# Three edits to a four-layer attention kernel: gates between layers 0 and 1, a mask added by TensorE, and a re-spread MLP product

## The reference, cut to what matters

```python
# layer 0: 16 heads of 16, keys and queries along t = 512, masked instance statistics of the values, then
#          x normalised by its own mean and variance and rescaled -> x1
# layer 1: 64-wide latents + context, 16 heads of 32, mask over the 256 context keys, out product,
#          residual, rmsnorm -> y1;  y1 -> 512x2048 product, gelu_tanh, 2048x512 product, + x1 -> x2
# layer 2: 32 query heads / 8 key heads of 16:
scores = einsum('bkgld,bksd->bkgls', q, k) * 0.25 + mask          # mask is 256x256 per batch
attn = softmax(scores); out = (attn @ v) @ Wo + bo
x3 = layernorm(out + x2)
# layer 3: position code, layernorm, 16 heads of 16 over t = 512, out product, layernorm, 2-product FFN
```

## Time and profile before

| | |
|---|---|
| time, median of 3 runs | 3267.26 us (3261.61 to 3276.46) |
| the profiled execution | 3280.75 us |
| its span, first to last instruction | 3279.0 us |
| busy: PE, DVE, ACT, POOL | 86%, 56%, 41%, 27% |
| mean granted clock of TensorE | 0.92 of 2.4 GHz |
| layer 0's scores L731 | from 84 to 681 us |
| layer 1's exponentials L1101 | from 782 to 1408 us |
| fc2 L862 | from 1410 to 2165 us |
| layer 2's scores L908 | from 1567 to 2384 us |

### The profile page before, as it was taken

How to read it: one execution, slowest core, us unless ns; L and a number is a source line. 1 busy time by engine, 2 the same in 40 slices (tenths; PEclk the granted TensorE clock), 3 DMA queues, 4 the chain that set the end, 5 groups by cost and what they waited for, 6 DMA issues and landing times. The chain is left out here.

```text
span 3279.0 us, 41359 instructions
## 1 busy us (share of the span) xinstructions
PE 2819.3 (86%) x14624; PEld 1322.2 (40%) x14624; DVE 1838.1 (56%) x4498; ACT 1339.5 (41%) x2342; POOL 882.9 (27%) x722
## 2 busy tenths in 40 slices
PE   4999998858999999989999999986678888888895
PEld 1222222224555555556555545542223333233332
DVE  3777777713444433212555565567867676667641
ACT  0566666632333333322334333322215544554562
POOL 1677777742444444310010001001111010100000
PEclk7999999979999999899999999987678899999997
DMA  4444444220002000121323332333333232323210
GB/s 99 102 103 103 109 100 102 62 94 33 27 27 83 27 28 24 66 79 42 68 59 62 63 65 55 68 63 88 66 91 80 67 78 58 90 58 71 69 32 20
DMA packets 182335, 219.93 MB, mean 67 GB/s; under 512 B 40840, under 2 KB 135664, under 8 KB 175984
## 3 DMA queue, kind: packets, MB, share of 16 engines
q1 hardware_dynamic: 170064, 189.74, 25.2%
q0 software_dynamic: 6016, 20.98, 1.9%
q10 hardware_dynamic: 6048, 6.56, 0.6%
HBM read 146.90 MB, written 51.64 MB: 61 GB/s over the span
## 5 line engine op out<-in xcount | busy, mean ns | idle before, releaser
L1480 DVE TENSOR_REDUCE l_M<-PS 128x1 f32<-128x512 f32 x512 | 334.4, 682 | 136.9 <-PE PS L967 134.0
L1260 DVE TENSOR_REDUCE l_M<-PS 128x1 f32<-128x512 f32 x512 | 331.8, 683 | 139.6 <-PE PS L722 138.8
L1199 ACT ACTIVATE l_P<-PS 128x512 f32<-128x512 f32 x512 | 286.3, 599 | 252.9 <-PE PS L977 235.4
L1563 POOL TENSOR_TENSOR l_S<-l_P 128x512 f32<-128x512 f32 x256 | 327.2, 1311 | 67.4 <-ACT l_P L1050 67.4
L1050 ACT ACTIVATE l_P<-PS 128x512 f32<-128x512 f32 x512 | 278.4, 598 | 103.5 <-PE PS L731 101.7
L967 PE MATMUL PS<-l_KS,l_QS 97*128 97x512 bf16 x512 | 207.9, 417 | 99.5 <-DVE l_M L1480 68.6
L1319 DVE TENSOR_REDUCE l1a_M<-PS 128x1 f32<-128x512 f32 x256 | 158.8, 681 | 203.6 <-PE PS L784 203.6
L1164 ACT ACTIVATE l_P<-l_P 128x1024 f32<-128x1024 f32 x128 | 135.3, 1057 | 301.8 <-DVE l_P L1400 301.6
L1386 DVE CUSTOM_DVE_ANT_0 l_JK<-PS,l_MK 128x256 f32<-128x256 f32 x512 | 195.5, 419 | 104.9 <-PE PS L897 102.8
L612 PE MATMUL PS<-l_YT,l_w_mlp_w 128*128 128x256 f32 x1024 | 240.0, 391 | 5.2 <-ACT l_YT L1126 5.1
L722 PE MATMUL PS<-l_KS,l_QS 97*128 97x512 bf16 x512 | 202.9, 406 | 42.9 <-DMA l_KS<-l_MB 19.7
(11 more groups left out here) (244 smaller groups left out, 4758.6 us busy)
## 6 DMA issues: line engine op xcount, KB each, us to landing
l_QS<-q_scratch SPq DMA_DIRECT2D x128, 128.0 KB, 5.7
q_scratch<-l_T SPq DMA_DIRECT2D x96, 128.0 KB
l_QS<-q_scratch SPq DMA_DIRECT2D x32, 384.0 KB, 5.0
k_scratch<-l_T SPq DMA_DIRECT2D x96, 128.0 KB
l_KS<-k_scratch SPq DMA_DIRECT2D x32, 384.0 KB
l_QS<-q_scratch SPq DMA_DIRECT2D x32, 256.0 KB, 5.6
l_KS<-k_scratch SPq DMA_DIRECT2D x32, 256.0 KB
l_RB<-l_recs SPq DMA_DIRECT2D x32, 256.0 KB
```

The lines of the kernel that those rows point to most:

```text
L1199: e.activation(t.P[quad % 4][:, m, :], PS[:, COUNTS.bank[st], :], ACT.Exp, scale=0.25).then_inc(q.sem("act.exp", st), 1)
L1260: e.tensor_reduce(t.M[i % 2][:, qt, hd:hd + 1], PS[:, COUNTS.bank[st], :], AX.X, ALU.max).then_inc(q.sem("dve.smax", st), 1)
L1480: e.tensor_reduce(t.M[i % 2][:, qt, hd:hd + 1], PS[:, COUNTS.bank[st], :], AX.X, ALU.max).then_inc(q.sem("dve.smax", st), 1)
L1563: x = e.tensor_tensor(t.S[j % 2][:, m, :], t.P[2 * j % 4][:, m, :], t.P[(2 * j + 1) % 4][:, m, :], ALU.add)
```

## The change

Layer 0 loses both barriers. Its steps keep their beats; layer 1 begins at beat 18.35, so its item 0 is projected while layer 0's item 15 has its scores made (beats 18.25 to 19.25). Gate 3 (ACT, POOL, SP; at 17.6, on mark 3 at 17.4) stands before layer 1's first weights; gate 4 (ACT, DVE, POOL, SP; at 19.6, on mark 4 at 19.4) before the rest (`1.start2`). PE passes no gate. The layouts of SBUF are rearranged so that what layer 1 touches early lies over what layer 0 has done with. The mask load becomes a step of its own (`1.mload`) with one DVE instruction instead of two. In layer 2 items 12 to 15 use `2.scm`: a second product, identity times the mask (fp32, 128x128 by 128x512), adds the mask in PSUM, and ACT takes the exponentials of 512 columns straight from there; DVE's addition is gone. `fc2`'s last four steps come 0.086 beats later, and six neighbours move a little. Some waits are renamed to fit.

```diff
-    return pipeline((a0, a1, a2, c, p), ((0.0, 1.0),) * 5, keep=True)
...
+    order = [(2 * b + h + beat + at, st) for b, h in ITEMS for beat, part in enumerate((a0, a1, a2, c, p)) for at, st in part(b, h)]
+    return order + [(-9, ("0.start", 0, 0, 0)), (17.4, ("mark", 3, 0, 0)), (19.4, ("mark", 4, 0, 0))]
...
+BEGIN1 = 18.35
...
-            at = -0.9 if b else 0.0
-            out += [(at, k("load")), (at + 0.15, k("mrow"))] + [((0.6 + at) if b else 0.05, k("lat", 0)), ((0.7 + at) if b else 0.08, k("lat", 1))]
+            out += [(-0.9 if b > 1 else -0.7, k("load")), (-0.6 if b else 1.2, k("mload")), (-0.5 if b else 1.27, k("mrow"))]
+            out += [(-0.3 if b else 0.0, k("lat", 0)), (-0.2 if b else 0.03, k("lat", 1))]
...
-        out += [(1.05 + 0.2 * n, k("smax", n)) for n in range(4)] + [(1.8, k("rows")), (1.81, k("turn"))]
+        out += [((1.05 + 0.2 * n) if (b, h) > (0, 0) else (1.46 + 0.1 * n), k("smax", n)) for n in range(4)] + [(1.8, k("rows")), (1.81, k("turn"))]
...
-    order = [x for x in order if first(x)] + [(1, ("barrier", 0, 0, 0))] + [x for x in order if not first(x)]
...
+    return order + [(-0.75, ("gate", 3, 0, 0)), (-0.74, ("1.start", 0, 0, 0)), (1.25, ("gate", 4, 0, 0)), (1.25, ("1.start2", 0, 0, 0)),
+                    (18.95, ("mark", 2, 0, 0))]
...
+MASK_PE = 12
+def score2(i):
+    return "2.scm" if i >= MASK_PE else "2.sc"
...
-            out += [(1.16 + 0.1 * j + 0.02 * (j // 4), k("fc2", j)) for j in range(8)]
-            out += [(2.2, k("cload")), (2.82, k("xt", 0)), (2.86, k("xt", 1))]
+            out += [(1.16 + 0.1 * j + 0.106 * (j // 4), k("fc2", j)) for j in range(8)]
+            out += [(2.18, k("cload")), (2.879, k("xt", 0)), (2.88, k("xt", 1))]
...
-        out += [(3.53, k("qproj", 0)), (3.55, k("qsplit", 0)), (3.61, k("qproj", 1)), (3.63, k("qsplit", 1))]
+        out += [(3.513, k("qproj", 0)), (3.55, k("qsplit", 0)), (3.61, k("qproj", 1)), (3.63, k("qsplit", 1))]
...
-            out += [(at, k("sc", 2 * n)), (at + 0.03, k("sc", 2 * n + 1)), (at + 0.06, k("exp", n))]
-        out += [(5.1 + 0.15 * n, k("vals", n)) for n in range(4)] + [(5.25, k("out", 0)), (5.58, k("out", 1))]
+            if score2(2 * b + h) == "2.scm":
+                out += [(at, k("scm", 2 * n)), (at + 0.03, k("scm", 2 * n + 1))]
+            else:
+                out += [(at, k("sc", 2 * n)), (at + 0.03, k("sc", 2 * n + 1)), (at + 0.06, k("exp", n))]
+        out += [(5.1 + 0.15 * n, k("vals", n)) for n in range(4)] + [(5.25, k("out", 0)), (5.608, k("out", 1))]
...
-            out += [(5.96, k("f0")), (6.15, k("f1", 0)), (6.24, k("f1", 1)), (6.66, k("guess"))]
+            out += [(5.96, k("f0")), (6.162, k("f1", 0)), (6.24, k("f1", 1)), (6.66, k("guess"))]
...
-         ("2.ksplit", "dve"): 0.02, ("2.qsplit", "dve"): 0.02, ("2.ksplit", "pool"): 0.04, ("2.qsplit", "pool"): 0.04,
+         ("2.ksplit", "dve"): 0.02, ("2.qsplit", "dve"): 0.02, ("2.ksplit", "pool"): 0.04, ("2.qsplit", "pool"): 0.052,
...
-GATED = {0: ("pe", "sp", "pool"), 1: ("pe", "sp"), 2: ("pe", "act", "dve", "pool", "sp")}
+GATED = {3: ("act", "pool", "sp"), 4: ("act", "dve", "pool", "sp"), 0: ("pe", "sp", "pool"), 1: ("pe", "sp"), 2: ("pe", "act", "dve", "pool", "sp")}
...
             elif kind == "1.smax":
-                q.wait_ge("pool.start", ("1.start", 0, 0, 0))
+                q.wait_ge("pool.start", ("1.start2", 0, 0, 0))
...
+                q.wait_ge("act.exp", ("0.sc", B - 1, 1, 31))
+                q.wait_ge("act.sums", ("0.sout", B - 1, 1, 1))
...
+            elif kind == "2.scm":
+                n, half = divmod(j, 2)
+                kv, kt = 2 * (n // 4) + n % 2, n // 2 % 2
+                q.wait_ge("mxa", step("2.turn", i))
+                bank = q.bank_empty(st)
+                e.matmul(PS[:, bank, :], t.K[b % 2][0:100, 4 * h + kv, kt * 128:kt * 128 + 128],
+                         t.Q[i % 2][0:100, 4 * kv + 2 * half:4 * kv + 2 * half + 2, :], start=True, stop=False,
+                         skip_group_check=True)
+                q.wait_ge("pool.mt", step("2.mt", 2 * b))
+                e.matmul(PS[:, bank, :].rearrange("p (b q) -> p b q", b=2), ident[:, :],
+                         t.MKT[:, kt:kt + 1, :].broadcast_to([128, 2, 256]), start=False, stop=True, skip_group_check=True
+                         ).then_inc(q.sem("pe.sc", st), 1)
...
+            elif kind == "2.scm":
+                n, half = divmod(j, 2)
+                q.wait_ge("pe.vals", step("2.vals", i, n // 2 - 2) if n > 3 else step("2.vals", i - 1, n // 2 + 2))
+                q.wait_ge("pe.sc", st)
+                e.activation(t.P[n % 4][:, 2 * half:2 * half + 2, :], PS[:, COUNTS.bank[st], :].rearrange("p (b q) -> p b q", b=2),
+                             ACT.Exp, scale=0.25).then_inc(q.sem("act.exp", st), 1)
```

More of the change, by code:

```diff
@@ L14 @@
 NEG = 1e30
[L19 to L56, removed]
 def layer0_order():
@@ L114, in steps @@
         return out
-    order = sorted([(2 * b + h + at, st) for b, h in ITEMS for at, st in steps(b, h)] + merge((tail[0], 0.0, 0.8)), key=lambda x: x[0])
-    first = lambda x: x[0] < 1 or x[1][0][0] == "0"
-    order = [x for x in order if first(x)] + [(1, ("barrier", 0, 0, 0))] + [x for x in order if not first(x)]
-    return order + [(18.95, ("mark", 2, 0, 0))]
+    order = [(2 * b + h + at, st) for b, h in ITEMS for at, st in steps(b, h)]
+    return order + [(-0.75, ("gate", 3, 0, 0)), (-0.74, ("1.start", 0, 0, 0)), (1.25, ("gate", 4, 0, 0)), (1.25, ("1.start2", 0, 0, 0)),
+                    (18.95, ("mark", 2, 0, 0))]
 BEGIN2 = 16.75
+MASK_PE = 12
+def score2(i):
+    return "2.scm" if i >= MASK_PE else "2.sc"
 def layer2_order():
@@ L183, in whole_order @@
 def whole_order():
-    o0, tail = layer0_order()
-    order = [(0, ("0.start", 0, 0, 0))] + o0 + [(0, ("1.start", 0, 0, 0))]
-    rest = [(BEGIN2 + at, st) for at, st in layer2_order()] + [(BEGIN2 + 18.3 + at, st) for at, st in layer3_order()]
-    o1 = layer1_order(tail)
-    n = o1.index((1, ("barrier", 0, 0, 0))) + 1
-    order += o1[:n] + sorted(o1[n:] + rest, key=lambda x: x[0])
+    places = ((0, layer0_order()), (BEGIN1, layer1_order()), (BEGIN1 + BEGIN2, layer2_order()),
+              (BEGIN1 + BEGIN2 + 18.3, layer3_order()))
+    order = sorted([(begin + at, st) for begin, steps in places for at, st in steps], key=lambda x: x[0])
     order += [(99, ("barrier", 0, 0, 0))]
@@ L356, in count @@
                         self.add(total, name, self.slot[name, st], st, 16 * n)
-            if st[0] == "mark" and st[1] < 0:
-                moved = {s: v for s, v in total.items() if "/" in s}
-            elif kind == "mark":
+            if kind == "mark":
                 self.marks.setdefault(st[1], {}).update(total)
             if kind == "barrier":
-                self.barrier.setdefault(st, {}).update({**total, **(moved or {})})
-                uses, moved = {}, None
+                self.barrier.setdefault(st, {}).update(total)
+                uses = {}
         self.total.update(total)
@@ L1333, in vector1 @@
             elif kind == "1.f1":
+                q.wait_ge("rows", ("1.start2", 0, 0, 0))
                 q.wait_ge("pe.f1", st)
@@ L1586, in gpsimd1 @@
                 e.dma_start(t.H[b % 2][:, :, 0:256], tokens(I["ctxT"][b])).then_inc(q.sem("inc", st), 16)
-                q.wait_ge("dve.mask", step("1.load", i - 2))
+            elif kind == "1.mload":
+                q.wait_ge("dve.mask", step("1.mload", i - 2))
                 e.dma_start(t.MI[:, :], I["mask1"][b:b + 1, :]).then_inc(q.sem("inm", st), 16)
@@ L1736, in sync1 @@
                 row(q, t.vb, "vb1")
+            elif kind == "1.start2":
                 row(q, t.ob, "ob1")
             elif kind == "1.mrow":
-                q.wait_ge("pool.start", ("1.start", 0, 0, 0))
+                q.wait_ge("pool.start", ("1.start2", 0, 0, 0))
                 q.wait_ge("pe.sc", step("1.sc", i - 3, 3))
-                q.wait_ge("dve.mask", step("1.load", i))
+                q.wait_ge("dve.mask", step("1.mload", i))
                 for m in range(4):
```

103 lines of the change are left out of this document (57 added, 46 removed), and 8 rows, old and new, of tables (FILLS, LATER, MOVES).

## The result

The changed kernel took 3222.89 us (median of 4 runs, 3218.19 to 3225.38) where the kernel before, in the same session, took 3271.86 (4 runs, 3261.61 to 3285.34): ratio 0.9839, 95% interval 0.9811 to 0.9867, 1.6% faster. The forecast was 3172, inside 3120 to 3225. So the sign and the range held, the range only just, and the forecast was 51 us too low. The profiled execution took 3225.38 us, its span 3223.6: 55.4 less than before, where the sum said 95. That trace of the kernel before is 8.9 us above the median of its four runs (3280.75 against 3271.86), so some of every gain that is read off against it is chance.

What follows compares the result with a forecast made beforehand. PE was taken as the bound in most of the kernel, with PE and DVE waiting for each other at layer 2's end. 57 + 35 + 3 = 95 us off 3280.75 gave 3186, less 13.5 for the median: 3172 us, range 3120 to 3225.

Steps and rivals of the forecast that it cites:

- Part 1: Joint of layers 0 and 1: layer 1's first score at 723 instead of 780.1, 57 us won, bounds 37 and 67.
- I take 14 us, and let the stretch grow by 6: Layer 0's last item: 14 of item 0's 20.4 us of transposes and projections fit there, lengthening the stretch by 6 us.
- 8 us free: Layer 0's last item, 643.5 to 683.5: by its busy time PE has only 8 us free.
- The 4 us set aside for gates: Joint: 4 us for gate 3 and for waits behind gate 4, near the low end.
- Whatever is won at an early place is kept: Most of the kernel: a PE that never idles passes an early gain on; layer 2's end is the exception.
- Part 2: Layer 2's body, the MLP's second product spread over the beat: 35 us won, bounds 10 and 45.
- the clock's term: Layer 2's output product: 5.40 us becomes 3.60, 1.8 us lost to the clock four times, 7.2 us won.
- The other hole: Layer 2's odd beat's end: 10.3 us of waits at the next item's maxima go, plus 7.5 for five other waits.
- Part 3: Layer 2's items 12 to 15, mask moved from DVE to PE: 3 us won, bounds 20 lost and 25 won.
- The join does nothing: Joint: each gate holds its engines about as long as the barrier did, 57 us stay, 3229 us; chance 0.05.
- The gates open late: Joint: transfers or loads delay gate 3 or 4 and PE stops; 25 us less, 3197 us; chance 0.18.
- Slower: Items 12 to 15: mask products run at half clock, all on the path, 118 us, giving 3293 us; chance 0.04.

Runs made afterwards that it cites:

- experiment 8: experiment 1 with layer 1's item 0 transposes and projections moved 0.87 of a beat later, behind layer 0's last scores; 3196.85 us, one run.
- experiment 1: Changed kernel with VectorE's split of the row maxima in layer 1 0.005 instead of 0.01 of a beat late, ahead of the value addition; 3206.42 us, ratio 0.9778.
- experiment 5: Changed kernel with GpSimd's last fold additions of layer 1's items 0 and 1 waiting for VectorE's split of the next item; 3207.93 us, one run.
- experiment 2: Changed kernel's joint of layers 0 and 1 alone, with the mask on VectorE and layer 2's beats as before; 3261.9 us, ratio 0.994.
- experiment 4: Changed kernel with the mask on VectorE in all 16 items; 3217.83 us, ratio 0.9808.
- experiment 11: Kernel before with the output product's first step at beat 6.162 instead of 6.15, behind the MLP's second product's first step; 3249.75 us, ratio 0.9923.
- experiment 3: Kernel before with only the change's layer 2 beats for the MLP's second product, its neighbours and GpSimd's split; 3231.5 us, ratio 0.9858.
- experiment 9: experiment 1 with layer 1's output weight and bias row loaded at beat 1.6 instead of 1.25, behind the mask rows; 3215.54 us, one run.
- experiment 10: Changed kernel with VectorE's split first, layer 1's item 0 projections late and the mask on VectorE in all items; 3193.16 us, ratio 0.9751.
- experiment 7: experiment 1 with the mask on TensorE from item 8 instead of 12; 3251.17 us, ratio 0.9926.
- experiment 12: experiment 10 with the mask on TensorE in items 14 and 15 only; 3192.88 us, ratio 0.9753.

## Why the prediction was right, and where it was wrong

**Part 1, 57 us forecast, 12.3 kept.** To layer 1's first score 27.1 us were won, 29.9 fewer than forecast; both figures lie outside this part's own bounds of 37 and 67. By the forecast's own steps:

- *"I take 14 us, and let the stretch grow by 6".* The step that failed. The stretch from item 15's first score to the last score grew from 30.0 to 46.8 us, 16.8; experiment 8 says 14.7 of it are the projections. That is 9 to 11 us missed. Its "8 us free" by busy time was near the truth, as 5.7 us were hidden; it was raised to 14 by an argument, not by a row. I had read the spare time from a stretch that began 8 us before item 15's scores and took the clock's shortfall as room.
- *The start of item 15's scores,* not in the sum at all: 7.7 us late, 3.2 of it already at its maxima (the two traces' layer 0 differ by that much anyway, as the experiments show) and 4.5 between. VectorE in order of time in the changed kernel shows where PE's wait of 2.8 us at 641.6 comes from:

```profile
640.83 0.17 DVE L1304 MEMSET l1a_MB<- 1x128 uint32 x1 [3.97 <-DMA l1a_row_vb<-in_rows]
640.92 0.62 DVE L1264 TENSOR_REDUCE l_M<-PS 128x1 f32<-128x512 f32 x1
```

  Layer 1's start makes VectorE wait for a bias row, and layer 0's maxima queue behind it. I had looked at which engines the gates hold, not at the wait inside the start itself. Moving it was not tried.
- *The gap behind the last score*, 35.4 forecast (688 to 723), 46.9 measured. The 4 us set aside for gates met 4.9 at the mask rows; not foreseen were the half clock behind that wait (25.8 us to the first score with three value steps in them, 23.4 in experiment 8 at clock 1.00 with five; by that some 5 us), the turn's 1.7, and about 3 for the last item's value product and shorter waits for ScalarE and VectorE. The sum of PE's work itself was right: in experiment 8, with all of item 0's 20.4 us in the gap, it lasts 54.8 against 31 + 20.4 = 51.4.
- *"Whatever is won at an early place is kept".* 14.8 us were not, as the step took PE for an engine that never idles in layer 1, and it idled for 5.6 and 5.3 us at two turns. Experiments 1 and 5 name the cause: the rounding put the split behind another operation, and there it ran beside GpSimd.

The transfers that the forecast feared at this place did come together: the stretch 640 to 650 has a DMA share of 1.02 and 362 GB/s. PE's one direct wait for a transfer behind it was 1.2 us; the 2.8 us above came through VectorE, from the bias row that moved in the same stretch. The Trainium skill (DMA: Bandwidth & Descriptors, Issuing engines are not separate DMA queues), by which the forecast put up to 11 us at stake, is neither borne out nor refuted by that.

**Part 2, 35 us forecast.** 36.8 between batch 0's and batch 7's second product in the two traces, 33.9 alone against the trace of before, 26.2 between experiments 2 and 4. Both holes are where the forecast had them. The output product in its new place, PE in order of time (compare):

```profile
1754.91 3.60 PE L846 MATMUL PS<-l_w_mlp_w,l_H 128*128 128x512 f32 x8
1758.34 3.60 PE L594 MATMUL PS<-l_w_Wo,l_AT 128*128 128x512 f32 x8
```

No wait for GpSimd, and 3.60 us in all five odd beats of the body, where it took 5.40 in four of five: the clock's term is real. Experiment 11 measures this hole at 15.6 to 23.8 us; the forecast's terms for it are 11.5 + 7.2 = 18.7. The whole alone does not settle whether to count the clock, on which the forecast had weighed the Trainium skill (TensorE: Matmul & The Clock Gate, What's actually happening): the waits alone are 13.9 us, with a fifth of 2.4 that the trace puts down to VectorE. The other hole, 10.3 + 7.5 = 17.8 forecast, gives 10.1. The loss that was named, the turn's transfers losing cover, came too: in the body 11.3 us in six waits of up to 2.0 (forecast "up to 3 us per batch"), while the 10.3 at the maxima went.

```profile
PE PS L892 <- DMA l_QS<-l_MT: 11.3, 6, 2.0
```

What the forecast missed is that part 2 also shortens items 12 to 15, by 11 us alone, by 15 between experiments 2 and 4. Which of its beats does it there, no run separates; the single beat of experiment 11 wins 4.1 in the same stretch.

**Part 3, +3 forecast, -6.3 measured,** inside its bounds of -20 and 25, with the wrong sign. The product itself was costed rightly: a score with its mask product takes 1.08 us at full clock (1.15 forecast). Wrong was the balance. VectorE gives 34 us of its time back (160 to 126, where the forecast took 43.7 off 149) and PE waits less for it, the waits of scores for its additions falling from 15.5 us to 0.6, yet the waits for the turn's transfers stay, and PE's busy time grows by 37. Who waits for whom over that stretch (PE; total, times, longest), the changed kernel and then experiment 4:

```profile
PE PS L900 <- DMA l_QS<-l_MT: 18.8, 4, 6.3
...
PE PS L892 <- DVE l_P L1405: 0.6, 3, 0.2
```

```profile
PE PS L892 <- DMA l_QS<-l_MT: 18.1, 4, 6.8
PE PS L892 <- DVE l_P L1405: 15.5, 11, 4.6
```

The middle of wide bounds was a guess, and the clock's rise from 0.75 to 0.90 did not pay for the rest.

**The rivals.** By time "The join does nothing" (3229) is nearest to the 3222.89 us, but it is not what happened: the gates did not hold the engines, and 27.1 us were won before 14.8 were lost elsewhere. "The gates open late" is nearest to what happened at the joint: its 25 us less put the time at 3197; the wait was as described, but short, and the rest had other causes. "Slower" had the mask products at the half clock: they began there (two in 1.9 us at 2147, in 1.02 us five us later) and did not stay. The sum as measured in the traces: 12.3 at the joint, 3.8 from there to batch 0's second product, 33.7 in layer 2's body, 10 in items 12 to 15, less 4.4 given back in layer 3.

That the time fell inside the range, by 2 us, was in part luck. Without the unforeseen 11 to 15 us of part 2 in items 12 to 15 it would have been about 3234 or more; without the tie that rounding broke it would have been near 3206, as in experiment 1. Of the signs that the forecast named, no wait over 5 us before the first score (4.9), none for GpSimd at the output product and 5.3 us won per batch held; 50 us at the first score (27.1) and VectorE near 105 us of 200 (123) did not, and in layer 2's body the turn's waits were new (11.3 us).

**Left open.** In the changed kernel layer 3 loses 6 us at its item 4, with PE at half clock behind a wait of 3.7 us for ACT; experiments 5 and 8 show 5 to 6 us there and experiment 3 at item 8, experiments 1, 4, 9 and 10 do not, though their layer 3 is the same and experiment 1 has that wait too. What differs is PE's wait for VectorE's maxima there, 5.6 us against 2.2; why is open. And 2 to 4 us are won between layer 1's items 13 and 15 in nine of the thirteen variants, part 2 alone among them, and none in experiments 5, 7, 9 and 12; I did not trace them.

## What to carry to other kernels

When an order is made by sorting sums of floating-point beats, an offset added to a whole group can swap steps that were tied: compare the orders of before and after, engine by engine, and keep tied steps apart by hand. Overlap two stages by placing the new work in the wait that the joint itself creates (here for the mask rows), not among work that already fills the engine, and look at every wait inside a moved start, since whatever its engine still has to do for the old stage queues behind it. Before moving work from a second engine to the first to balance them, measure the price where the first sets the pace: here 0.90 us for each product of 0.925.

## What the runs showed of the hardware that was not expected

VectorE operations of 0.19 us took 2.28 and 2.36 us beside GpSimd additions of 2.34 us, in one case a copy-like one with a single input in SBUF (fp32 to bf16, 16 columns), in the other one with two. Kept apart they took 0.19 and 0.18, wherever they stood.
